# Attention and FFN layer on one core: half of the value product in high and low parts, with GpSimd making the low parts

## The reference, cut to what matters

```python
xn = layernorm(x)
q, k, v = split(xn @ w_qkv.T)                      # 16 heads of 128
q, k = rope(q), rope(k)
attn = softmax(einsum('bqhd,bkhd->bhqk', q, k) * scale)
out = einsum('bhqk,bkhd->bqhd', attn, v)           # the value product
y = x + out @ w_out.T + ffn(xn)
```

## Time and profile before

| | |
|---|---|
| time, median of 3 runs | 2508.67 us (2503.35 to 2509.61) |
| the profiled execution: its time | 2508.02 us |
| its span from first to last instruction | 2506.2 us |
| TensorE busy | 2457.5 us, 98% |
| VectorE busy | 1982.2 us, 79% |
| ScalarE busy | 1437.6 us, 57% |
| GpSimd busy | 1392.9 us, 56% |
| share of the 16 DMA engines taken by packets | 59.9% |

### The profile page before, as it was taken

One profiled execution on the slowest core, in us unless ns is written; L12 is line 12 of the kernel. 1 busy time (PEld: TensorE's weight loads), 2 busy tenths in 40 slices (PEclk: granted clock), 3 DMA queues, 4 the chain that ended last, 5 costly groups with the idle time before them and its releaser, 6 DMA issues. The chain is left out here.

```text
span 2506.2 us, 41398 instructions
## 1 busy us (share of the span) xinstructions
PE 2457.5 (98%) x12656; PEld 2139.8 (85%) x12656; DVE 1982.2 (79%) x3204; ACT 1437.6 (57%) x2648; POOL 1392.9 (56%) x1115
## 2 busy tenths in 40 slices
PE   6999999999999999999999999999999999999899
PEld 4888888888888888888888888888888888888688
DVE  6877878787887878788787878878787887878576
ACT  5656666565656566565656556655555566565233
POOL 6567656665655555565556555655555565555031
PEclk9999999999999999999999999999999999999999
DMA  4665666656665555656665655656575565655842
GB/s 135 167 168 151 173 159 161 172 157 189 179 163 147 151 153 153 157 146 188 173 164 143 160 150 151 159 146 185 152 183 146 151 159 152 158 140 144 231 141 68
DMA packets 267289, 396.28 MB, mean 158 GB/s; under 512 B 38496, under 2 KB 120800, under 8 KB 267104
## 3 DMA queue, kind: packets, MB, share of 16 engines
q1 hardware_dynamic: 267232, 395.67, 59.9%
HBM read 91.43 MB, written 35.65 MB: 51 GB/s over the span
## 5 line engine op out<-in xcount | busy, mean ns | idle before, releaser
L1020 PE MATMUL o_ps<-keys_first,v_rows 128*128 128x256 f32 x4096 | 930.9, 381 | 10.4 <-DMA keys_first<-turned_blocks 10.4
L1020 PEld LDWEIGHTS o_ps<-keys_first,v_rows 128*128 128x128 f32 x4096 | 767.7, 191 | 110.4 <-DMA keys_first<-turned_blocks 11.6
L1020 PE MATMUL s_ps<-seq_parts 128*128 128x512 f32 x3072 | 834.3, 409 | 12.7 <-ACT probs L689 8.0
L792 DVE TENSOR_REDUCE neg_max<-s_ps 128x1 f32<-128x1024 f32 x512 | 611.3, 1203 | 160.3 <-PE s_ps L1020 160.1
L689 ACT ACTIVATE probs<-s_ps,neg_max 128x1024 f32<-128x1024 f32 x512 | 568.7, 1111 | 247.9 <-DVE neg_max L792 241.7
L1020 PEld LDWEIGHTS s_ps<-seq_parts 128*128 128x128 f32 x3072 | 577.9, 189 | 133.6 <-ACT probs L689 12.1
L804 DVE STREAM_TRANSPOSE turned_blocks<-probs 128x512 f32<-128x512 f32 x1024 | 662.9, 685 | 32.2 <-ACT probs L689 10.3
L558 POOL TENSOR_TENSOR rope_a<-rope_a,cos 128x512 f32<-128x512 f32 x250 | 324.6, 1298 | 633.1 <-ACT rope_b L673 633.1
L563 POOL TENSOR_TENSOR seq_parts<-rope_a,seq_parts 128x512 fp32r<-128x512 f32 x250 | 320.5, 1282 | 288.4 <-ACT seq_parts L680 288.4
L1020 PE MATMUL slot_ps<-seq_parts,w_parts 128*128 128x512 f32 x1506 | 386.9, 392 | 4.8 <-DMA seq_parts<-xnt_parts 4.8
L680 ACT ACTIVATE seq_parts<-rope_a 128x512 fp32r<-128x512 f32 x250 | 157.6, 630 | 387.9 <-POOL rope_a L561 386.4
(11 more groups left out here) (111 smaller groups left out, 1733.6 us busy)
## 6 DMA issues: line engine op xcount, KB each, us to landing
keys_first<-turned_blocks SPq DMA_DIRECT2D x2048, 128.0 KB, 2.7
w_parts<-w_qkv_parts SPq DMA_DIRECT2D x72, 512.0 KB, 4.3
seq_parts<-xnt_parts SPq DMA_DIRECT2D x14, 1024.0 KB, 8.3
w_qkv_parts<-w_parts SPq DMA_DIRECT2D x24, 512.0 KB, 3.7
wo_parts<-w_out_parts SPq DMA_DIRECT2D x48, 256.0 KB, 3.1
w_raw<-in_w_qkv SPq DMA_DIRECT2D x24, 256.0 KB, 4.3
y<-in_x SPq DMA_DIRECT2D x16, 256.0 KB, 3.3
ln_x<-in_x SPq DMA_DIRECT2D x16, 256.0 KB, 3.4
```

Of the source, the lines that this page charges most:

```text
L792: nc.vector.tensor_reduce(neg_max[:, k2 % 16:k2 % 16 + 1], s_ps[k2 % 2][:, :], AXX, ALU.max, negate=True).then_inc(max_ready, 1)
L1020: ins = nc.tensor.matmul(out, w, m, start=(n == 0), stop=(n == len(terms) - 1))
```

## The change

1. Value product. Of the 8 key tiles of a chunk the first 4 (`SPLIT = 4`) are now multiplied in parts, the other 4 unsplit as before. `values` issues 8 matmuls with the high parts of the probabilities (`v_hi` and `v_lo` by `p_hi`), waits for the low parts, then issues 4 matmuls `v_hi` by low, then the 4 unsplit ones.
2. Parts of the probabilities. At the end of its step ScalarE waits for the keys of this chunk and copies four key tiles (1024 elements a partition) to `p_hi` (`probs_high`). At the beginning of its next step GpSimd subtracts them in place in two instructions of 512 elements, front and back (`probs_low`). `BACK_BY_DVE` is empty, so VectorE makes none of these.
3. Parts of v. ScalarE's copy of the first four tiles goes to `v_hi`; VectorE makes `v_lo` (`v_low`), two instructions for a pair.
4. Order of the keys. The keys within a head are stored by their remainder modulo 4: the sums of k halves (not of q halves) are read with a step of 4 elements (`by_remainder`) by `rotated_high` on ScalarE and by the low part on GpSimd. In return `turn` is one transpose of 128x1024 for a tile that reads without a step, where there were two of 128x512 that read every second element. `low_out` and `high_out` lose their rearranged accesses.
5. Moves. `move_tile` brings one tile in 4 DMAs (pieces of 1 KB), as soon as this tile is turned; `move_chunk` waited for both tiles and brought both in 8 DMAs (pieces of 2 KB). The first tile of chunk k+1 is turned and moved at the end of step k.
6. Rotation. `rotate_rest` is divided into `rotated_sum` (three instructions) and `rotated_low` (one), which usually stands one step later, and the groups change places: q and k go earlier, v later.
7. Layer norm. ScalarE now makes mean and normalisation (`mean`, `normalise`), VectorE no longer; the parts of `quantise` are spread over more steps.

```diff
+SPLIT = 4
...
-        GROUPS = {(3, 0): (0, "qk0", 0), (3, 1): (1, "qk0", 1), (4, 0): (2, "qk0", 2), (4, 1): (3, "v", 0),
-                  (5, 0): (4, "qk0", 3), (6, 0): (5, "v", 1), (6, 1): (6, "v", 2), (7, 0): (7, "qk1", 0),
-                  (7, 1): (8, "qk1", 1), (0, 0): (9, "qk1", 2), (0, 1): (10, "v", 3), (1, 0): (11, "qk1", 3)}
+        GROUPS = {(2, 1): (0, "qk0", 0), (3, 1): (1, "qk0", 1), (4, 0): (2, "qk0", 2), (4, 1): (3, "v", 0),
+                  (5, 0): (4, "qk0", 3), (6, 0): (5, "v", 1), (6, 1): (6, "qk1", 0), (7, 0): (7, "v", 2),
+                  (7, 1): (8, "qk1", 1), (0, 0): (9, "qk1", 2), (0, 1): (10, "qk1", 3), (1, 0): (11, "v", 3)}
...
+        FRONT, BACK = slice(0, 2), slice(2, SPLIT)
+        BACK_BY_DVE, BACK_BY_POOL = (), (0, 1, 2, 3, 4, 5, 6, 7)
...
+        def by_remainder(a):
+            return a.rearrange("p (j k b) -> p j b k", k=QUAD, b=QUADS)
...
+            def probs_low(c, k):
+                slot = k % 2
+                pool.wait_ge(p_hi_ready, c + 1)
+                low = keys_first[:, slot, :, FRONT, :]
+                nc.gpsimd.tensor_tensor(low, low.bitcast(F32), p_hi[:, slot, :, FRONT, :].bitcast(F32),
+                                        ALU.subtract).then_inc(p_lo_front, 1)
+                if k % 8 in BACK_BY_POOL:
...
+                if not (first and k == 0):
+                    probs_low(c - 1, k - 1)
+                if k8 == 0:
+                    if not first:
+                        rotated_low(p, "qk1", 0)
+                        rotated_sum(p, "qk1", 1)
+                    rotated_sum(p, "qk1", 2)
+                if k8 == 1:
+                    if not first:
+                        rotated_low(p, "qk1", 1)
+                    rotated_low(p, "qk1", 2)
+                    rotated_sum(p, "qk1", 3)
+                if k8 == 2:
+                    rotated_low(p, "qk1", 3)
+                if k8 == 3 and more_pairs:
+                    rotated_sum(p + 1, "qk0", 0)
+                if k8 == 4 and more_pairs:
+                    rotated_low(p + 1, "qk0", 0)
+                    rotated_sum(p + 1, "qk0", 1)
+                if k8 == 5 and more_pairs:
+                    rotated_low(p + 1, "qk0", 1)
+                    rotated_sum(p + 1, "qk0", 2)
+                if k8 == 6 and more_pairs:
+                    rotated_low(p + 1, "qk0", 2)
+                    rotated_sum(p + 1, "qk0", 3)
+                    rotated_low(p + 1, "qk0", 3)
+                if k8 == 7 and more_pairs:
+                    rotated_sum(p + 1, "qk1", 0)
...
+            def probs_high(i, k):
+                act.wait_ge(keys_moved[k % 4], chunk_moves(i, k))
+                nc.scalar.activation(p_hi[:, k % 2], keys_first[:, k % 2, :, 0:SPLIT, :].bitcast(F32),
+                                     ACT.Copy).then_inc(p_hi_ready, 1)
...
+                for kt in range(SPLIT):
+                    nc.tensor.matmul(out, v_hi[:, parity, kt, cols], p_hi[:, slot, :, kt, :], start=(kt == 0), stop=False)
+                    nc.tensor.matmul(out, v_lo[:, parity, kt, cols], p_hi[:, slot, :, kt, :], start=False, stop=False)
+                pe.wait_ge(p_lo_front, c + 1)
...
+                for kt in range(SPLIT):
+                    nc.tensor.matmul(out, v_hi[:, parity, kt, cols], keys_first[:, slot, :, kt, :], start=False, stop=False)
```

More of the change, by code:

```diff
@@ L240, in group_at @@
                 return None
[L241 removed]
+            ahead = k // 8 + (1 if k % 8 >= 2 else 0)
             if last and ahead > 1:
@@ L602, in step @@
                 p = i * 2 + k // 8
+                more_pairs = not (last and k >= 8)
                 more = splitting and not (isinstance(p, int) and p + 1 >= PAIRS_PER_SEQ)
+                if not (first and k == 0):
+                    probs_low(c - 1, k - 1)
+                if k8 == 0:
[24 more added lines that the diff above has]
+                    rotated_sum(p + 1, "qk1", 0)
+                if k == 2:
+                    guess(i + 2, LN_COLS)
                 if k8 == 0 and more:
@@ L613, in step @@
                     wo_low(p + 1, 0)
-                if k == 2:
-                    guess(i + 2, LN_COLS)
-                for slot in (0, 1):
-                    g = group_at(k, slot, last)
-                    if g and g[1] != "v":
-                        p = i * 2 + g[3]
-                        rotate_rest(p, g[1], g[2])
             steps_splitting(pool, step)
@@ L938, in _ @@
             row_max(1, 1)
+            for (place, part, n), bank in zip(FIRST_GROUPS, FIRST_BANKS):
+                if part == "v" and n in V_SPLIT:
+                    v_low(0, 0, n, bank)
+            turn(0, 0, 0, True)
             def step(i, k, first, last):
@@ L945, in step @@
                 if not tail:
-                    turn(i, k, 0, first)
+                    turn(i, k, 1, first)
                 if has_out:
                     low_out(c - 2, k % 2)
-                if not tail:
-                    turn(i, k, 1, first)
+                if (k - 1) % 8 in BACK_BY_DVE and not (first and k == 0) and not (last and k == 17):
+                    probs_low(c - 1, k - 1)
+                g = None if tail or (first and k == 0) else group_at(k - 1, 1, last)
+                if g and g[1] == "v" and g[2] in V_SPLIT:
+                    v_low(i * 2 + g[3], g[3] % 2, g[2], slot_ps[:, 1])
                 if (k - 1, 1) == LN_SLOT:
@@ L960, in step @@
                     row_max(t + 3, 2 * k + 3)
+                g = None if tail else group_at(k, 0, last)
+                if g and g[1] == "v" and g[2] in V_SPLIT:
+                    v_low(i * 2 + g[3], g[3] % 2, g[2], slot_ps[:, 0])
                 if has_out:
```

248 lines of the change are left out of this document (173 added, 75 removed).

## The result

| | before | after |
|---|---|---|
| time, median of 4 runs each | 2508.09 us (2503.35 to 2509.61) | 2628.09 us (2620.53 to 2636.62) |
| the profiled execution: its time, its span | 2508.02, 2506.2 us | 2620.53, 2618.7 us |

The change makes the kernel slower by 4.8%: the ratio is 1.0483, 95% interval 1.0447 to 1.0519. The direction was forecast, the size was not: 27 us were forecast and 120 us came, 112.5 between the two profiled executions, beyond the range.

A forecast was written before the change was run, and what follows sets the result against it. TensorE bound the kernel before; afterwards a GpSimd-ScalarE loop: 71.1 + 0.8 + 1.1 = 73.0 us a pair against 72.4. 24 pairs lose 14 us, seven weight-splitting pairs 13: 2508.02 plus 27 gives 2535 us, range 2485 to 2600.

The forecast's parts named there:

- the ring: GpSimd's low parts wait for ScalarE's `probs_high`, made behind the rotated high, which waits for GpSimd's sum; 71.1 us a pair.
- step 7: Eighth step of a pair's loop: 8.2 us; TensorE's wait for q's rotated low part was expected here.
- The allowance of 0.8 us: Per pair: 0.4 for longer single instructions, 0.2 for the layer norm's `guess`, 0.2 for VectorE's late transposes.
- TensorE's saving: Value product in parts: 0.30 us saved a chunk, 2.4 a pair; TensorE alone would need 70.0 a pair, about 2431 us.
- steps 1, 5 and 6: Steps of a pair's loop: 9.5 us for 1 and for 5, 10.6 for 6, before any price for strided reads.
- GpSimd's strided read: Rotated low part reading `rope_a` with a 16-byte step: 0.27 us each, four on the loop, 1.1 us a pair.
- Strided reads cost on both engines: Rival: ScalarE's `rotated_high` pays too, 0.44 us each, 1.3 a pair; 75 us a pair, 2610; chance 0.17 for 2575 and more.
- I cost that at nothing too, except at step 2: Keys' DMAs: issued in 4 instead of 8, so landing earlier; no cost except four issues and landing, 4.6 us, in one step.
- Steps 2 and 3: Steps of a pair's loop: 2 is 3.75 us on GpSimd but 4.1 because the chunk's keys come later; 3 is 8.2.
- at nothing, with TensorE and GpSimd as its cover: VectorE: one longer transpose pays for `v_low`, layer norm given away; stays below nine tenths busy, so no cost.
- step 0: First step of a pair's loop: GpSimd's own work, 2.50 + 1.25 + two sums of 3.87 = 11.5 us.
- a ring of 72.2 to 72.6: Rival that the two effects cancel: a pair about as long as before, 2501 to 2516 us; chance 0.14.

The follow-up runs named there:

- experiment 6: Changed kernel plus two tiny SyncE transfers ahead of the first tile's key moves in every chunk, behind the same buffer wait: 2673.31 us, ratio 1.0671 to the kernel before.
- Experiment 4: Changed kernel, VectorE making the back half of low parts in every other step: first kernel 2636.84 us; second, subtraction moved between the two row maxima, 2593.42 us.
- experiments 2, 3 and 8: Changed kernel: `probs_high` ahead of rotated high in five steps, 2573.38 us; unstrided reads, both engines 2564.7, ScalarE alone 2605.84; ScalarE order, VectorE between maxima, one filling matmul, 2553.81.
- experiment 2: Changed kernel with ScalarE's `probs_high` ahead of the rotated high part in steps 0, 3, 4, 5 and 7: 2573.38 us, ratio 1.0287 to the kernel before.

## Why the prediction was right in kind and wrong in size

The mechanism that the prediction put its forecast on, the ring, is the one that sets the pace. The step that failed is the length of this ring: 73.0 us for a late pair, where 76.0 came. Three costs on it stood at nothing: ScalarE's strided reads (0.52 us for each, three in a pair), the keys' moves outside step 2, and TensorE's clock behind its wait at step 7 (1.3 us in 18 of 31 pairs). The allowance of 0.8 us did not cover them. Term by term:

- **TensorE's saving: right.** 0.28 us of a chunk in the timeline, 0.30 forecast, and TensorE alone no longer set the pace.
- **The ring: right.** It was foreseen from the order of two programs, and exchanging two lines on ScalarE took 55 us off. Its arithmetic holds where nothing else joins in: steps 1, 5 and 6 are within 0.2 us. GpSimd's wait for `probs_high` is 1.69 us in step 5 and 2.21 in step 4, where ScalarE's read has its step; 1.9 was forecast for both.
- **GpSimd's strided read: right.** 0.27 was chosen as the middle between 0 and 0.55, and 1.55 - 1.28 = 0.27 us came; that the middle was hit so exactly is luck. The estimate from the Trainium skill ("GPSIMD Engine Reference", "7. Performance pitfalls for Q7 kernels"), 0.43, was too high here: the measurement decides.
- **"Strided reads cost on both engines" stood only among the rivals: the first term that failed.** Its mechanism came true, at 0.52 us on ScalarE (upper bound forecast 0.44), three on the ring: 1.5 us a pair by its own price. The low bound of 0 was kept for an operation that no row showed, though the same read was given 0.27 on GpSimd. The Trainium skill's note in "SBUF — State Buffer" on cachelines says that reads need two hits on a line for the full rate; both engines' rows agree with it.
- **"I cost that at nothing too, except at step 2", of the keys' moves: failed.** "a tile is issued in 4 instead of 8 for both, so it lands earlier" overlooked that the first tile's moves also wait for their buffer, so that eight issues stand in a row as before. Steps 2 and 3 are 0.85 and 1.3 us over the forecast (0.5 of the latter is ScalarE's strided read), and experiment 6 shows the issues on the path in step 2. In step 3 they add 0.28 for 0.86; what else holds step 3 is not settled.
- **VectorE "at nothing, with TensorE and GpSimd as its cover": failed as a reason.** It stands between the scores and the exponential, with ScalarE's two copies queued behind. Experiment 4 prices the place of one subtraction at 43 us; what VectorE costs in the change itself no run isolates.
- **TensorE's wait at step 7 was named, what follows it was not.** The wait is 2.6 us in the mean, 79.9 in all, and by itself costs step 7 nothing: behind it step 7 takes 8.62 us, close to the 8.2 forecast and 0.5 for ScalarE's read. The halved clock behind 18 of the 31 waits costs 1.3 us each time. With two matmuls in the wait 32 us come back.
- **The allowance of 0.8 for all that a ring must carry was too small.** The sum of a late pair, 73.0 forecast and 76.0 measured: +1.5 ScalarE's reads, +0.85 step 2, +0.8 step 3, +0.7 step 7 (the last two beyond the strided read; that of step 7 is the low clock in 13 of the 22 pairs), +0.3 step 0, -0.4 steps 4 to 6, -0.8 the allowance that these replace. This adds up, but the terms are not independent: experiments 2, 3 and 8 all gave less than their sum.
- **Two smaller slips.** A late pair of before takes 72.6 in the mean and not 72.4, which makes the forecast 5 us too high. And a ring of 72.2 to 72.6 gives, with the prediction's own prices for early pairs, 2510 to 2523 and not 2501 to 2516; the forecast itself does not hang on it.

What stays open: why step 0 takes 0.3 us more than GpSimd's own work, and what sets step 3 apart from the issues. In the kernel of experiment 2 GpSimd waits there, in step 0, 1.18 us a pair for a group's copy (0.18 in the changed kernel), which says that step 0 has its own limit on the way from TensorE, but no run isolates it.

## What to carry to other kernels

Before work is moved from a full engine to idle ones, write down the loop that it closes between their in-order programs, and count in it everything that stands in the same queues: a read with a step, DMA issues, a reduction that an exponential waits for. Busy shares of 79% and 68% were already the limit here, and the same change at half the size (two tiles) gained 1% where the full one lost 4.8%. A term for which no row exists deserves the same middle value on every engine that performs it.

## What the runs showed of the hardware

- A read of fp32 with a step of 16 bytes, 512 elements a partition: ScalarE 1.15 instead of 0.63 us, GpSimd (one strided input of two) 1.55 instead of 1.28.
- VectorE and GpSimd hold each other up when both subtract in SBUF: 1.27 instead of 0.68 us and 2.01 instead of 1.55. In the first kernel of experiment 4 the 19 subtractions of VectorE beside an idle GpSimd took 0.68 each, the 109 others 1.30 in the mean.
- Behind a wait of 2.81 us TensorE's granted clock was 0.50 for 3.4 us. So it was behind 18 of 31 waits in this place; behind seven others of 2.65 to 3.14 us it stayed at 1.00. Each time the step got 1.3 us longer. Two extra matmuls in the wait made the kernel faster by 32 us.
- Two issues of a transfer of a few KB took 0.81 us of SyncE's queue, where two of the 128 KB ones take about 1.3 (eight in 5.16 us).
